# Two-layer decoder on one core: a home of its own for the key and value weight of the second cross attention, scaling on GpSimd ahead of the feed-forward, and ScalarE's copies and roundings put elsewhere

## What is computed

```
x = x + attn0(layernorm(x))            # 32 heads of 64, window 64, sinks, output 2048 -> 512
x = x + xattn0(layernorm(x), ctx)      # latent queries against a context of 375 tokens
x = x + ffn0(layernorm(x))             # h = bitlinear(x, w_fc); gelu; bitlinear(h, w_proj)
x = x + attn1(layernorm(x))            # 16 heads of 128, output 2048 -> 512
x = x + xattn1(layernorm(x), ctx)      # qp = q @ Wq.T;  k, v = split(ctx[:, :112] @ Wkv_expand.T)
x = x + moe(layernorm(x))              # 8 experts, twice
...
bitlinear(x, w): xn = layer_norm(x); g = max|xn| per row
                 clip(xn * 128 / g, -128, 128) * g / 128  @  ternary(w)
```

## Time and profile before

| what | us |
|---|---|
| median of 3 runs | 1641.29 (1640.02 to 1643.6) |
| the profiled execution | 1637.46 |
| its span, first to last instruction | 1635.6 |
| PE busy | 1580.2 (97%) |
| DVE busy | 936.4 (57%) |
| ACT busy | 732.2 (45%) |
| POOL busy | 663.8 (41%) |

### The profile page before, as it was taken

How to read it: one execution, slowest core, us unless ns; L and a number is a source line. 1 busy time by engine, 2 the same in 40 slices (tenths; PEclk the granted TensorE clock), 3 DMA queues, 4 the chain that set the end, 5 groups by cost and what they waited for, 6 DMA issues and landing times.

```text
span 1635.6 us, 24562 instructions
## 1 busy us (share of the span) xinstructions
PE 1580.2 (97%) x9834; PEld 1346.3 (82%) x9834; DVE 936.4 (57%) x1532; ACT 732.2 (45%) x1231; POOL 663.8 (41%) x482
## 2 busy tenths in 40 slices
PE   9999999999999999899999989998989999999998
PEld 8997667778899998778889976877778888888887
DVE  7555663456544464687668566353666445554554
ACT  3114654222687765665511156333545334353342
POOL 3974441530598863421137633112433322222221
PEclk9999999999999999999999999999999999999999
DMA  4110003133222006200002100110011111111111
GB/s 169 65 65 16 2 2 133 40 114 122 91 72 64 14 29 250 86 1 1 1 14 65 52 27 1 50 39 27 21 33 50 48 52 59 41 50 46 56 54 45
DMA packets 28581, 88.52 MB, mean 54 GB/s; under 512 B 4155, under 2 KB 4283, under 8 KB 28216
## 3 DMA queue, kind: packets, MB, share of 16 engines
q1 hardware_dynamic: 28468, 86.96, 15.8%
HBM read 85.11 MB, written 1.84 MB: 53 GB/s over the span
## 4 chain that ended last, share of the span: by engine, by line
PE 84%; DVE 7%; ACT 4%; issue 4%; POOL 1%; DMA 0%; ACTq 0%; DVEq 0%; POOLq 0%
PE PS L261 19%; PE PS L263 18%; PE PS L262 18%; PE PS L266 7%; PE PS L1162 5%; PE PS L1499 3%; PE PS L1514 2%; PE PS L598 2%; PE PS L989 1%; PE PS L622 1%; PE PS L1746 1%; PE PS L1734 1%; PE PS L588 1%; PE PS L606 1%; POOL HL L310 1%
## 5 line engine op out<-in xcount | busy, mean ns | idle before, releaser
L310 POOL TENSOR_TENSOR HL<-stg,HL 128x1024 fp32r<-128x1024 f32 (+2 forms) x110 | 241.6, 2198 | 508.2 <-ACT HL L305 490.1
L261 PE MATMUL PS<-XT,HL 128*128 128x448 f32 x608 | 224.0, 368 | 0.7 <-POOL HL L310 0.6
L263 PE MATMUL PS<-XT,HL 128*128 128x448 f32 x608 | 222.1, 365 | 0.0
L262 PE MATMUL PS<-XT,HL 128*128 128x448 f32 x608 | 222.0, 365 | 0.0
L305 ACT ACTIVATE HL<-stg 128x1024 fp32r<-128x1024 f32 (+2 forms) x111 | 104.5, 944 | 211.8 <-PE PS L263 196.4
L261 PE MATMUL PS<-HL,XT 128*128 128x512 f32 (+1 forms) x380 | 137.2, 361 | 2.1 <-POOL HL L310 1.3
L263 PE MATMUL PS<-HL,XT 128*128 128x512 f32 (+1 forms) x380 | 134.2, 353 | 0.0
L262 PE MATMUL PS<-HL,XT 128*128 128x512 f32 (+1 forms) x380 | 134.0, 353 | 0.0
L261 PEld LDWEIGHTS PS<-XT,HL 128*128 128x128 f32 x608 | 114.2, 188 | 12.5 <-POOL HL L310 1.0
L262 PEld LDWEIGHTS PS<-XT,HL 128*128 128x128 f32 x608 | 114.3, 188 | 9.0
L263 PEld LDWEIGHTS PS<-XT,HL 128*128 128x128 f32 x608 | 114.2, 188 | 9.1
(11 more groups left out here) (321 smaller groups left out, 3802.8 us busy)
## 6 DMA issues: line engine op xcount, KB each, us to landing
stg<-in_wst SPq DMA_DIRECT2D x87, 512.0 KB, 3.3
stg<-in_wst SPq DMA_DIRECT2D x16, 352.0 KB, 3.1
stg<-in_wst SPq DMA_DIRECT2D x16, 320.0 KB, 3.1
wsum<-in_wfc SPq DMA_DIRECT2D x8, 512.0 KB, 3.6
wsum<-in_wpj SPq DMA_DIRECT2D x8, 512.0 KB, 3.5
raw<-in_wfc SPq DMA_DIRECT2D x8, 512.0 KB, 6.3
stg<-in_wst SPq DMA_DIRECT2D x16, 256.0 KB, 2.6
raw<-in_wpj SPq DMA_DIRECT2D x7, 512.0 KB, 7.4
```

The costliest lines, as they stand in the source:

```text
L261: e.matmul(out, lh, rh, start=start, stop=False)
L262: e.matmul(out, lh, rl, start=False, stop=False)
L263: return e.matmul(out, ll, rh, start=False, stop=stop)
L310: e.tensor_tensor(slot(k)[:, 1, 0:n], stg[k % NSTG][:, 0:n], slot(k)[:, 0, 0:n].bitcast(F), A.subtract).then_inc(*done(*low_part(k)))
```

## The change

- Stream: `kv2` moves ahead of `q2`, and belongs to `WHOLE`. It is rounded by ACT into W2, a place of its own in the memory of QO, behind the loop of `act_o1` and a wait for the last `o_lo`; POOL subtracts into W2. q2 0 is rounded after the high part of tile 0, q2 1 ahead of the root of tile 6.
- `pe_q2`: keys, then values 0 and 1, then the four queries; the turn of the last tile after the first query. Queries go to a place Q2. On DVE the value copies come ahead of the low part of the last tile; the mask copy of ACT stays behind its last query copy.
- o2 pieces are rounded and subtracted at w = 1 and 3.
- The scaling of `quant_scale` moves from DVE to POOL, ahead of the clip. Tiles 1 and 3 turn into banks 1 and 3, for which n = 1 and n = 3 of the first step wait.
- Two roundings and subtractions (the second and third q1 piece) move from the end of `act_ox` and `pool_ox` to steps 4 and 5 of the feed-forward.
- `key_query_out` comes ahead of `ln_root`; the turn of the last tile in `pe_q` ahead of kc = 2 of half 0.

```diff
@@ -50,7 +50,7 @@
...
     kinds += [("o1", i) for i in range(8)]
-    kinds += [("q2", i) for i in range(2)] + [("kv2", 0)] + [("o2", i) for i in range(2)]
+    kinds += [("kv2", 0)] + [("q2", i) for i in range(2)] + [("o2", i) for i in range(2)]
     for n in range(8):
@@ -64,7 +64,7 @@
...
 WIDTH = {"kq": 704, "ox": 640, "sw": 512}
-WHOLE = ("kq", "qx")
+WHOLE = ("kq", "qx", "kv2")
@@ -187,6 +187,8 @@
...
         KC = at("KC", [128, 2, NB, S], R, QOX)
+        Q2 = at("Q2", [128, NB, 4, S], F, rQO)
+        W2 = at("W2", [128, 2, PW], R, rQO + 14336)
         K2 = at("K2", [128, 4, T], F, rKV)
@@ -829,13 +831,13 @@
...
             for t in range(NT):
+                if t in (3, 5):
+                    key_query_out(e, t // 2 - 1)
                 ln_root(e, "lnx", t)
...
                     key_hi(e, 1)
-                if t in (3, 5):
-                    key_query_out(e, t // 2 - 1)
                 if t == 5:
@@ -977,11 +979,12 @@
...
                     elif half:
-                        ln_turn(e, "lnx", NT - 1, xn[0], NT - 1)
                         e.wait_ge(*upon("dve_ln", "lnx", NT - 1, "lo"))
...
                     for kc in range(4):
+                        if hp == 0 and half == 0 and kc == 2:
+                            ln_turn(e, "lnx", NT - 1, xn[0], NT - 1)
                         hs = slice(half * HT, (half + 1) * HT)
@@ -1345,13 +1348,14 @@
...
             e.wait_ge(*upon("dve_fq", "rmax", t))
-            e.tensor_scalar(z, z, qrs[:, k, 6:7], -128.0, A.mult, A.mult).then_inc(*done("dve_fq", "q", t))
             e.wait_ge(*upon("act_fq", "root", t))
...
         def quant_clip(e, t):
-            z = xz[t % 4][:, :]
-            e.wait_ge(*upon("dve_fq", "q", t))
+            k, z = t % 4, xz[t % 4][:, :]
+            e.wait_ge(*upon("dve_fq", "rmax", t))
+            e.tensor_scalar(z, z, qrs[:, k, 6:7], -128.0, A.mult, A.mult).then_inc(*done("pool_fq", "q", t))
+            e.wait_ge(*upon("pool_fq", "q", t))
             e.tensor_scalar(z, z, 128.0, -128.0, A.min, A.max).then_inc(*done("pool_fq", "y", t))
@@ -1374,12 +1378,12 @@
...
         def q_bank(t):
-            return 7 if t < 4 else t
+            return 7 if t in (0, 2) else t
...
             e.wait_ge(*upon("pool_fq", "y", t))
-            if t < 4:
-                e.wait_ge(*(upon("dve_fq", "lo", t - 1) if t else upon("dve_ox", "v", OX - 1)))
+            if t in (0, 2):
+                e.wait_ge(*(upon("dve_fq", "lo", 0) if t else upon("dve_ox", "v", OX - 1)))
             turn4(e, xz[t % 4], q_bank(t)).then_inc(*done("pe_fq", t))
@@ -1426,7 +1430,7 @@
...
             for c in range(OX):
-                if c < OX - 1:
+                if c < OX - 3:
                     round_w(e, first_ox + c + 4)
@@ -1456,7 +1460,7 @@
...
         def pool_ox(e):
-            for c in range(OX):
+            for c in range(OX - 2):
                 rest_w(e, first_ox + c + 3)
@@ -1507,6 +1511,8 @@
...
                             e.wait_ge(*upon("dve_fq", "lo", f))
+                        elif st == 0 and n in (1, 3):
+                            e.wait_ge(*upon("dve_fq", "lo", n))
                         if st:
@@ -1561,6 +1567,8 @@
...
                     e.activation(rsl[:, p % 2, 1:2], mvl[:, p % 2, 1:2], ACT.Sqrt, bias=eps[:, 0:1], scale=1.0).then_inc(*done("act_ln", "lnf", p, "root"))
+                if st in (4, 5):
+                    round_w(e, first_ox + OX + st - 3)
@@ -1632,6 +1640,8 @@
...
                 e.tensor_scalar(osc[:, t, 3:4], rs[:, k, 2:3], rs[:, k, 6:7], gam[:, 1, 5:6], A.mult, A.mult).then_inc(*done("pool_f", "osc", t))
+                if t in (4, 5):
+                    rest_w(e, first_ox + OX + t - 3)
@@ -1823,19 +1833,24 @@
...
                 o_hi(e, "o1", c + 4)
-                if c % 2:
+                if c % 2 and c < 11:
                     round_w(e, o1 + c // 2 + 3)
...
                     e.activation(KC[:, 0, :, :], kc_[:, :, :], ACT.Copy).then_inc(*done("act_o1", "kc"))
+            k = piece["kv2", 0][0]
+            e.wait_ge(*upon("dve_o1", "lo", 15))
+            e.wait_ge(*upon(f"sp_stg{k % NSTG}", k))
+            e.activation(W2[:, 0, :], stg[k % NSTG][:, :], ACT.Copy).then_inc(*done("act_kv2"))
             for t in range(NT):
                 if t == NT - 1:
-                    round_w(e, o1 + 9)
                     round_w(e, o1 + 10)
...
                     ln_hi(e, "ln2", t - 1, t - 1)
+                if t == 1:
+                    round_w(e, o1 + 9)
@@ -1851,7 +1866,13 @@
...
             o1 = piece["o1", 0][0]
-            for k in range(o1 + 3, o1 + 11):
+            for k in range(o1 + 3, o1 + 8):
+                rest_w(e, k)
+            k = piece["kv2", 0][0]
+            e.wait_ge(*upon("act_kv2"))
+            e.tensor_tensor(W2[:, 1, :], stg[k % NSTG][:, :], W2[:, 0, :].bitcast(F), A.subtract).then_inc(*done("pool_kv2"))
+            freed[k] = ("pool_kv2",)
+            for k in range(o1 + 9, o1 + 11):
                 rest_w(e, k)
@@ -1868,61 +1889,53 @@
...
             e.wait_ge(*upon("pe_q2", "q", u))
-            e.activation(q_at(half, 0, 2 * i + e_), psv(bank), ACT.Copy).then_inc(*done("act_q2", u))
+            e.activation(Q2[:, 4 * half:4 * half + 4, 2 * i + e_, :], psv(bank), ACT.Copy).then_inc(*done("act_q2", u))
         def key2(e, c, half, bank):
-            w = slot(piece["kv2", 0][0])
-            mm3(e, PS[:, bank, 0:HT], w[:, 0, c * 128:(c + 1) * 128], w[:, 1, c * 128:(c + 1) * 128],
+            mm3(e, PS[:, bank, 0:HT], W2[:, 0, c * 128:(c + 1) * 128], W2[:, 1, c * 128:(c + 1) * 128],
                 KC[:, 0, 4 * half:4 * half + 4, :], KC[:, 1, 4 * half:4 * half + 4, :], True, True).then_inc(*done("pe_q2", "k", c, half))
...
         def value2(e, b, bank):
-            k = piece["kv2", 0][0]
-            w = slot(k)
-            mm3(e, PS[0:S, bank, :], KC[:, 0, b, :], KC[:, 1, b, :], w[:, 0, 512:1024], w[:, 1, 512:1024], True,
+            mm3(e, PS[0:S, bank, :], KC[:, 0, b, :], KC[:, 1, b, :], W2[:, 0, 512:1024], W2[:, 1, 512:1024], True,
                 True).then_inc(*done("pe_q2", "v", b))
-            if b == NB - 1:
-                freed[k] = "pe_q2", "v", b
...
-        K_BANK, Q_BANK = (7, 0, 1, 2), (3, 7, 0, 1)
+        K_BANK, Q_BANK = (7, 0, 1, 2), (7, 0, 1, 2)
         def pe_q2(e):
-            has_w(e, piece["kv2", 0][0])
+            e.wait_ge(*upon("pool_kv2"))
             e.wait_ge(*upon("dve_o1", "kc"))
...
                 key2(e, c, 0, K_BANK[c])
-            e.wait_ge(*upon("dve_ln", "ln2", 3, "lo"))
+            for b in range(2):
+                e.wait_ge(*upon("dve_ln", "ln2", 3 + b, "lo"))
+                value2(e, b, 3 + b)
             for u in range(4):
-                if u:
-                    e.wait_ge(*upon("act_q2", "k", u - 1))
+                e.wait_ge(*upon("act_q2", "k", u))
                 query2(e, u, Q_BANK[u])
-                if u == 1:
+                if u == 0:
                     ln_turn(e, "ln2", NT - 1, xn[0], NT - 1)
-            e.wait_ge(*upon("act_q2", "k", 3))
-            value2(e, 0, 2)
-            e.wait_ge(*upon("dve_ln", "ln2", 4, "lo"))
-            value2(e, 1, 4)
...
             query2_out(e, 0, Q_BANK[0])
+            ln_hi(e, "ln2", NT - 1, NT - 1)
             query2_out(e, 1, Q_BANK[1])
-            ln_hi(e, "ln2", NT - 1, NT - 1)
             query2_out(e, 2, Q_BANK[2])
...
         def dve_q2(e):
+            value2_out(e, 0, 3)
+            value2_out(e, 1, 4)
             ln_lo(e, "ln2", NT - 1, NT - 1)
-            value2_out(e, 0, 2)
-            value2_out(e, 1, 4)
@@ -1942,7 +1955,7 @@
...
                         p = slice(32 * i, 32 * i + 32)
-                        last = e.matmul(PS[0:S, i, c * S:(c + 1) * S], QO[p, 1 + 2 * w, c, :], K2[p, c, w * S:(w + 1) * S],
+                        last = e.matmul(PS[0:S, i, c * S:(c + 1) * S], Q2[p, w, c, :], K2[p, c, w * S:(w + 1) * S],
                                         start=False, stop=True, skip_group_check=True)
@@ -2061,8 +2074,8 @@
...
                     turned(2 * w - 2)
-                if w in (2, 4):
-                    round_w(e, piece["o2", w // 2 - 1][0])
+                if w in (1, 3):
+                    round_w(e, piece["o2", w // 2][0])
                 if w == NB:
@@ -2109,8 +2122,8 @@
...
                     share8(e, "a2", 2 * w)
-                if w in (2, 4):
-                    rest_w(e, piece["o2", w // 2 - 1][0])
+                if w in (1, 3):
+                    rest_w(e, piece["o2", w // 2][0])
                 if w == NB:
...
```

## The result

The kernel after takes 1622.66 us (median of 4 executions, 1621.89 to 1623.05), the kernel before beside it 1641.38 us (1640.02 to 1643.6). The ratio is 0.9884, with a 95% interval from 0.9867 to 0.9901. The profiled execution of after took 1622.37 us with a span of 1620.6 us.

The account below looks back on a forecast made before the run. TensorE, busy 97% of the span, was taken as the bound, leaving 55.4 us idle to win. Gains 1.9 + 0.8 + 3.1 + 7.1 + 1.3 = 14.2 us took 1641.3 to 1627.1 us, range 1623.0 to 1632.0.

Parts of the forecast that it names:

- Parts A and B: First output projection and start of latent queries: earlier Cf copy gains 1.9 us, last tile's turn inside half 0 gains 0.8.
- Part C: Quantizing tiles ahead of the feed-forward: scaling on GpSimd, own banks, two roundings later; gain 3.1 us.
- the ramp: Feed-forward: chain from centring to PE's restart is ScalarE's and VectorE's alone and shifts as a whole, 17 us.
- the bank wait: Quantizing tiles: PE's 2.63 us wait for bank 7 goes; 1.1 us become a longer wait at st = 2.
- cost 0: Two roundings moved to feed-forward steps 4 and 5, some 1 us of ScalarE each: absorbed where it idles.
- Part D: Start of second cross attention: key and value weight rounded early into W2, 5.55 us wait gone; gain 7.1 us.
- Part E: Step 5 of the second cross attention: PE's 1.25 us wait for an o2 piece goes; gain 1.3 us.
- rival 1: Clock at 730 to 740: second low stretch, 1628.8 us, or the existing one falls away, 1625.4; chance 0.08 each.
- The ramp is not bound by the table load: Rival 2, feed-forward: ScalarE's table load bounds the ramp, part C worth 1.3 not 3.1, 1628.9 us; chance 0.10.
- the queries do not wait inside: Rival 3, part D: queries wait for key copies or weights, half of 7.1 us returns, 1630.7 us; chance 0.05.
- GpSimd's scale is far from 5.2 us: Rival 4, quantizing tiles: per-row scale on GpSimd needing 5.2 us makes the kernel slower, 1644.6 or more; chance 0.02.
- theory 1: From the experiments: PE gaps can be followed by 1.2 GHz stretches, more in ordinary executions of before; explains the rest of the gain.

Follow-up runs that it names:

- the fourth of before: The unchanged kernel before, profiled once more as its fourth execution: 1643.21 us, idle 55.6 us, PE busy 1585.7 us.
- the kernel after measured again: The kernel after, unchanged, timed again beside a kernel before of 1639.38 us: 1623.09 us (1621.05 to 1625.57), ratio 0.9901.
- the first with four fills: The kernel before with unread matmuls meant for four PE waits, those for Cf running behind the wait: 1637.66 us beside 1640.49, ratio 0.9982.
- the second execution of before: The unchanged kernel before, profiled a second time: 1637.85 us, idle 55.5 us, PE busy 1580.6 us.

## Why the prediction was right in its steps and wrong in its time

**Parts A and B** (forecast 2.7). Right: 3.1 us of idle time alone. The wait for xn came to 0.64 us (forecast 0.75), half 1 has none.

**Part C** (3.1). Right in size: 3.2 at the restart. The scale takes 0.69 us, inside the bounds of 0.49 to 1.2; the ramp is 16.9 us (forecast 17); the bank wait moved to step 2 as said. Incomplete in its reason: the forecast put the roundings at "cost 0" and gave their move no gain. With the scaling alone the wait for the bank fell by nearly the 1.3 us credited, but GpSimd's queue, not cleared of subtractions, gave 0.4 us back at the first turn, and only 0.8 came.

**Part D** (7.1). Right in the profiled execution. From the first key product to the mask matmuls PE takes 15.10 us (1095.30 to 1110.40); the forecast, 1101.84 to 1116.95, was 15.11. 5.3 of the 7.1 is idle time, the rest mostly the low stretch behind the wait (1.4 us). In other executions that stretch costs more, 1.2 us more in the fourth of before.

**Part E** (1.3). Right: 1.3 us of idle time.

**The sum and the clock.** The profiled executions are 15.1 us apart (1637.46 less 1622.37), for 14.2 forecast. The excess is the low stretch at 730, which fell away (1.7 us); rival 1 had named it, with a chance of 0.08. That it fell away in this execution is luck: the kernel after measured again shows it at 720. Against it stand 0.9 us by which after is late ahead of 330, from the odd wait at the start: 14.2 + 1.7 - 0.9 = 15.0.

**The step that failed** is the last one: "The median of the runs shown is 3.8 us above it; the trace doesn't say why, and I take the distance as constant." It isn't constant. In before it is mostly made of low-clock stretches that vary between executions: idle time is 55.4 to 55.6 us throughout, busy time 1580.2 to 1585.7, and the profiled execution was one with few of them. 1.5 us of busy time in two of the four is the slower pace at full clock, which the change does not touch. In after the median lies 0.3 us from the profiled execution.

The 18.7 us are 11.2 to 12.4 us of waits and 6.3 to 7.5 of other time. Part of the latter is the small sample: 1641.38 is the median of four executions, and the 91 timed later have 1640.2. Beside a before of 17 executions the kernel after gained 16.3 us, which leaves 4 to 5 for the clock, of which the sum had counted about 1.8. The mean clocks give the same size as an estimate: 0.996 became 0.9995, and in before 0.001 goes with some 1.2 us.

Had the whole distance been taken as gone, the forecast would have been 1637.5 - 14.2 = 1623.3, as the text itself worked out for the profiled execution. That would have been right within 0.7 us, in part by luck, for the pace and the sample do not go away with gaps. The range took in the scatter of a median, but not the case that the scatter has a cause which the change removes. Its lower end, 1623.0, does not follow from its terms either: 1625.4 less 1.3 is 1624.1. The median measured again, 1623.09, lies just inside, so it is the gain, 16.3 and 18.7 for 14.2, that shows the miss, more than the 0.3 us under the range.

**The rivals.** The ramp is not bound by the table load; the queries do not wait inside; GpSimd's scale is far from 5.2 us. **Still open** is which gap is followed by low clock in a given execution. The fills say that an idle PE is needed at the place, not that it is enough, and with one gap filled low stretches were still seen behind others (at 331, at 724), so that the medians fell by less than theory 1 expected, or not at all. Open too is the slower pace between 46 and 124 us.

## What to carry to other kernels

Split a profiled time into PE's busy and idle time before forecasting, and look at more than one execution, at the mean clock of each beside its time. If the busy time differs while the idle time doesn't, look for windows of low clock; what they account for is tied to PE's gaps, and a change that removes gaps removes it too. The rest has another cause, as the slower pace here. Before moving an operation to another engine, look at what stands ahead of it in that engine's queue; here the queue took back 0.4 of the 1.2 us that the move of the scaling gained. Take the base of a forecast from many executions: four of them lay 1 us above the median of 91. A wait that can't be removed can be filled with matmuls that nobody reads, provided that they start when the wait starts and end before it does. Each fill restored the clock at its place, but of the six kernels with fills two had a median clear of its reference, by 1.6 us (the long wait filled in before) and 2.8 (the first with four fills).

## What the runs showed of the hardware

- The time of one unchanged kernel varies with the low clock behind its gaps: 1637.46 to 1643.21 us in four profiled executions, 5.7 us, or 0.35% of the span, in a kernel whose PE is 97% busy. About 4 of the 5.7 are the clock, 1.5 a slower pace at full clock.
- Low clock stood behind waits as short as 0.97 us (at 1134.19, in the fourth execution of before) and was absent in some executions behind 2.00 and 2.63 us; behind the wait of 5.55 us it was never absent. Where a gap was filled, no execution that was profiled showed it there.
- A low stretch that falls partly into the gap costs less. In the second execution of before the windows 1100 and 1110 stand at 0.73 and 0.93, 3.4 us of lost clock, in the profile of before at 0.86 and 0.97, 1.7 us; PE's busy time differs by 0.4 us only, and the rest lay in the gap, where it costs nothing.
- At a granted clock of 1.00 matmuls of 448 columns start 0.203 us apart in most profiled executions, and 0.207 apart from about 46 to 124 us in four of the 20.
- GpSimd scales 128x512 by a per-row factor in 0.69 us, against 0.61 for its clip and 0.49 for VectorE's scaling of the same shape.
